# Layer norm rows and betas from VectorE to ScalarE, and old states added by TensorE as a product with the unit matrix

## The chip, the cores and the metric

The kernel runs on one core of a Trainium2 chip. The metric is the time on the device in microseconds; lower is better. The core has TensorE (matmuls, results to PSUM), VectorE and ScalarE (elementwise work on SBUF and PSUM), GpSimd (no PSUM) and SyncE (here only DMA issues). Each engine runs its own instructions in the order in which they are written, and they wait for each other by semaphores. All numbers are fp32.

## The reference, cut to what matters

```python
def _L0_attn_ref(x, ...):                      # x: layer normed, (2, 2048, 256); 16 heads of 64
    xn = layernorm(x) * ln_w + ln_b
    q, k, v = xn @ Wq.T, xn @ Wk.T, xn @ Wv.T
    alpha, aR = sigmoid(xn @ Wa.T + ba), sigmoid(xn @ WaR.T + baR)     # a gate for each key element
    beta, gamma = sigmoid(xn @ Wb.T + bb), sigmoid(xn @ Wg.T + bg)     # one for each head
    def step(carry, inp):                      # over the 2048 tokens
        S, R = carry                           # two states of 64x64 for each head
        kn = k_t / norm(k_t)
        r = clip(v_t - S.T @ kn, -1, 1)
        S = a_t[..., None] * S
        S = S + b_t * outer(kn, v_t - kn @ S)
        R = aR_t[..., None] * R
        R = R + g_t * outer(kn, r - kn @ R)
        return (S, R), S.T @ q_t + R.T @ q_t
    return os @ Wo.T + residual

x = x + _layernorm(_L0_attn_ref(_layernorm(x), ...))
x = x + _layernorm(_L0_ffn_ref(_layernorm(x), ...))   # router, 8 of 64 experts, and a shared expert
```

## The kernel before

The sequence is cut into 32 chunks of 64 tokens. A chunk holds both batches, so a tile has 128 rows. Within a chunk the recurrence is written as matrix products. With decayed keys it is solved by the inverse of a triangular 64x64 matrix for each head and state, then the states S and R (16 units of 128x64 each in SBUF) are carried to the next chunk. After attention come one last tile of routing and then the experts, 320 tiles in a pipeline of their own; the change doesn't touch the experts.

`attention` (from L490) writes out the program of each engine, chunk by chunk, in an order set by hand. While a chunk n is worked on, the front of chunk n+1 is made in the gaps: norm, projections, gates, keys, triangles A. The norms and the routing of the chunk n−1 run beside that.

PSUM has eight banks. `order_of_jobs` (L64) lists all results that go there in the order in which TensorE makes them. The table `SMALL` rotates through six banks, `WIDE` through two, and each names the engine that empties the bank. A result may begin only when the result six (or two) places ahead of it was emptied. By this list W follows six places behind U, RU behind SU, OUT behind the first half of RU, and the first half of V behind the second half of RU.

The parts of a chunk's end, in TensorE's order, with their names:

- U (L690) and PR, its product with the queries (L692). SU (L695) is the update of S, product of the keys kT and U. NS (L700) sums the squares of the next chunk's keys; ScalarE makes the norms of it in place (`key_norms`, L457), and VectorE multiplies the keys by them (L859).
- O (L702) is the output. Its first part uses the old S and R, and its end sets O_begun. SD is the shared expert. W (L711) is the solution for R, copied by ScalarE to B (L1049); with it O is finished (L713), and RU (L716) is the update of R.
- A (`triangles`, L591) are the triangles of the next chunk. VectorE masks them (`masked`, L758), ScalarE and GpSimd copy their diagonals to D (L922, L1063), and the next chunk's transposition (L778) needs these. RK ranks tokens for the routing, `route_pages` (L340) on VectorE follows it. OUT (L728) is the projection of the output and is added by VectorE to the residual (L887). V (L731) are the values of the next chunk.

VectorE adds SU to S after O_begun (L869) and RU to R (L878). ScalarE then multiplies each of 16 units by its decay (`decay_state`, L951): S after the copies of W and O, R behind the diagonals.

In the front half, from L778, VectorE inverts the triangles in 30 steps (`invert_steps`, L431), with other work set between them: four layer norms (y, the rows for the router, x of the chunk n+2, and xhat). Of each, VectorE makes the mean and the variance (`ln_stats`), ScalarE the inverse deviation by Ln and Exp (`ln_guess`, L916), and VectorE the row (`ln_apply`, L751). Between them stand the subtraction of KS, the masks of PQ (L809) and RQ, and the betas, 1 / (1 + exp) by an add and a reciprocal (L816). Its last step writes N (L827), for which TensorE's Z waits. ScalarE takes the exponentials of the gates (`exp_gate`, L929) and the copies of projections in this half; TensorE's projections rotate through the two wide banks, so each waits for ScalarE.

## Time and profile before

| | |
|---|---|
| median of three runs | 3295.07 us (3291.97 to 3296.05) |
| profiled execution | 3276.76 us, its span 3274.9 us |
| TensorE matmul busy | 2773.5 us, 85% |
| VectorE busy | 2721.3 us, 83% |
| ScalarE busy | 1943.8 us, 59% |
| GpSimd busy | 953.5 us, 29% |
| mean granted TensorE clock | 0.906 |

Attention fills the span up to some 2540 us, and the experts the rest from about 2620 us. The 40 slices of the page show VectorE at 8 to 9 tenths in nearly all of attention. A matmul's end is modelled, so TensorE's busy share is not its share at its peak. In timelines, a row has its start, its length, engine, line and names; "x2" says that two instructions are merged, and the bracket is the idle time of the engine ahead of it and who ended it. A matmul of fp32 shows as two instructions in the trace, so 32 matmuls of the program are x64 there.

### The profile page before, as it was taken

The numbers are of one execution on the slowest core, as the hardware profiler recorded it, in microseconds if no ns is written. First come the engines' busy times: TensorE is split into PE (matmuls) and PEld (weight loads), VectorE is DVE, ScalarE is ACT, GpSimd is POOL, SyncE is SP. The second block draws the span as 40 slices with busy tenths as digits, with TensorE's granted clock in tenths as the row PEclk, the third lists the DMA queues.
The fourth block names the chain that finished last, engine by engine and source line by source line (L and its number), as shares of the span: only waits on it lengthen the run. The fifth ranks groups of instructions, "written<-read, shape, count | busy, mean of one in ns | idle before, by whom it ended". The sixth has DMA issues, their size and how long they took to land. (4 is left out here: it accounts for less than half of the span.)

```text
span 3274.9 us, 132532 instructions
## 1 busy us (share of the span) xinstructions
PE 2773.5 (85%) x55642; PEld 2460.6 (75%) x55642; DVE 2721.3 (83%) x6827; ACT 1943.8 (59%) x5180; POOL 953.5 (29%) x928
## 2 busy tenths in 40 slices
PE   3888888888888888888888888888886199999986
PEld 3878888887787888788788888888786177777664
DVE  2889898888989988999999999999997156777776
ACT  2656555556666655666666555666654077666664
POOL 3112222222222222223222222233221101444444
PEclk8988898888888988989999899999998599999998
DMA  3321111111111111111111111111110945777776
GB/s 116 82 64 37 36 35 35 35 35 37 39 35 35 37 37 35 43 35 35 39 40 41 35 35 35 35 42 35 39 40 30 347 144 170 221 217 224 220 217 180
DMA packets 209563, 264.55 MB, mean 81 GB/s; under 512 B 30673, under 2 KB 183250, under 8 KB 208210
## 3 DMA queue, kind: packets, MB, share of 16 engines
q1 hardware_dynamic: 183936, 188.53, 19.0%
q0 software_dynamic: 24576, 67.27, 7.2%
q8 instruction: 450, 7.37, 1.0%
q14 instruction: 135, 1.11, 0.1%
q10 hardware_dynamic: 466, 0.27, 0.0%
HBM read 125.37 MB, written 130.58 MB: 78 GB/s over the span
## 5 line engine op out<-in xcount | busy, mean ns | idle before, releaser
L379 POOL DMA_INDIRECT table<-tail,places x256 | 277.1, 1082 | 721.1 <-DVE BR L852 214.8
L1496 PE MATMUL bank<-w,tail 128*128 x1280 | 357.2, 401 | 31.4 <-ACT tail L1539 14.5
L1468 POOL DMA_INDIRECT tail<-y_table,places x256 | 249.5, 975 | 449.3 <-DMA y_table<-tail 314.0
L1091 POOL COPY inv_r<-N 32x512 f32<-32x512 f32 x128 | 136.4, 1065 | 734.0 <-DVE N L827 730.0
L445 DVE TENSOR_TENSOR tri<-tri,step 128x58 f32<-128x58 f32 (+13 forms) x896 | 305.5, 341 | 30.8
L444 DVE TENSOR_TENSOR step<-tri 128x58 f32<-128x58 f32 (+13 forms) x896 | 301.4, 336 | 26.4
L1496 PEld LDWEIGHTS bank<-w,tail 128*128 128x128 f32 x1280 | 219.2, 191 | 95.9 <-issue 72.7
L1586 DVE TENSOR_TENSOR more<-tail 128x1 f32<-128x1 f32 x320 | 50.8, 159 | 193.7 <-ACT tail L1548 189.6
L1511 PE MATMUL bank<-w,tail 128*128 x640 | 191.1, 380 | 2.7 <-DVE tail L1597 1.4
L1546 ACT ACTIVATE tail<-bank 128x129 f32<-128x129 f32 x320 | 89.8, 281 | 158.9 <-PE bank L1496 156.3
L1482 PE MATMUL bank<-ident,tail 128*128 128x128 f32 x640 | 125.1, 278 | 66.1 <-DMA tail<-table 65.6
L587 PE MATMUL bank<-xnT,wa 128*128 128x128 f32 x992 | 125.3, 287 | 50.2 <-ACT xnT L970 50.2
L572 PE MATMUL bank<-B,kT_r 64*64 64x64 f32 x2048 | 107.2, 294 | 63.1 <-DVE S L869 63.1
L587 PEld LDWEIGHTS bank<-xnT,wa 128*128 128x128 f32 x992 | 119.4, 201 | 54.4 <-ACT xnT L970 54.4
L768 DVE TENSOR_TENSOR_SCAN c<-restart,z 128x1024 f32<-128x1024 bf16 x62 | 158.3, 2592 | 0.0
L1597 DVE TENSOR_SCALAR tail<-bank,more 128x256 f32<-128x256 f32 x320 | 152.1, 475 | 2.8 <-DMA y_table<-tail 2.1
L1482 PEld LDWEIGHTS bank<-ident,tail 128*128 128x128 f32 x640 | 78.8, 142 | 100.1 <-DMA tail<-table 78.3
L934 ACT ACTIVATE z<-bank,neg_bias 128x128 f32<-128x128 f32 x496 | 137.9, 374 | 27.0 <-PE bank L587 23.1
L572 PEld LDWEIGHTS bank<-B,kT_r 64*64 64x64 f32 x2048 | 102.3, 206 | 68.2 <-DVE S L869 68.2
L1539 ACT COPY tail<-bank 128x256 f32<-128x256 f32 x320 | 119.6, 374 | 56.7 <-PE bank L1482 56.0
L1068 POOL COPY T<-L_s 32x512 f32<-32x512 f32 x64 | 38.7, 605 | 368.2 <-DVE L_s L763 366.8
L955 ACT ACTIVATE S<-S,dec_end 128x64 f32<-128x64 f32 x512 | 125.8, 335 | 30.4 <-DVE S L869 30.4
(275 smaller groups left out, 8103.8 us busy)
## 6 DMA issues: line engine op xcount, KB each, us to landing
table<-blank SPq DMA_DIRECT2D x320, 128.5 KB, 3.2
tail<-table SPq DMA_DIRECT2D x320, 128.5 KB
y_table<-tail SPq DMA_DIRECT2D x320, 128.0 KB
w<-in_wpack_dram SPq DMA_DIRECT2D x16, 1540.0 KB, 19.3
tail<-in_x_dram SPq DMA_DIRECT2D x66, 64.0 KB, 2.5
x_rows<-tail SPq DMA_DIRECT2D x32, 128.0 KB
sh_rows<-tail SPq DMA_DIRECT2D x32, 128.0 KB, 1.9
table<-tail,places POOLq DMA_INDIRECT x256, 2.9
```

The lines of the kernel that those rows point to most:

```text
L379: nc.gpsimd.indirect_dma_start(out=table, out_offset=bass.IndirectOffsetOnAxis(ap=t.places[:, TOP * (n - 1) + k:TOP * (n - 1) + k + 1], ax ...
L444: link(nc.vector.tensor_tensor(step, s[:, 0:k, k:k + 1].broadcast_to([P, k, rest]), over(s[:, k, k + 1:Q], k), ALU.mult))
L445: link(nc.vector.tensor_tensor(s[:, 0:k, k + 1:Q], s[:, 0:k, k + 1:Q], step, ALU.add))
L572: mm = nc.tensor.matmul(ps[r, C * i:C * i + C], lhsT(r, u), rhs(r, u), start=(m == 0), stop=(m == len(pairs) - 1))
L587: mm = nc.tensor.matmul(ps[:, P * m:P * m + P], w[:, kt, P * hp:P * hp + P], t.xnT[:, kt, :], start=(kt == 0), stop=(kt == 1))
L768: nc.vector.tensor_tensor_scan(t.c[:, gate, :, :].rearrange("p u n -> p (u n)"), t.restart[:], t.z[:, gate, :], 0.0, ALU.mult, ALU.add).th ...
L934: ins = nc.scalar.activation(t.z[:, gate, P * hp:P * hp + P], ps[:, P * m:P * m + P], ACT.Exp, bias=t.neg_bias[:, gate, hp:hp + 1], scale= ...
L1468: nc.gpsimd.indirect_dma_start(out=t.term[2 * (m % 2) + k], out_offset=None, in_=d.y_table[0:P * closed(b) + P + 1, :], in_offset=bass.Ind ...
L1482: mm = nc.tensor.transpose(t.ps[T_bank[i % 2]][:, P * kt:P * kt + P], t.x_slot[i % X_RING][:, P * kt:P * kt + P], t.ident[:, :])
L1496: mm = nc.tensor.matmul(ps[:, 0:257], t.xT_slot[i % 3][:, P * kt:P * kt + P], weights(i, 257 * kt, 257), start=(kt == 0), stop=(kt == 1))
L1511: nc.tensor.matmul(t.ps[y_bank[i % 2]][:, 0:256], t.hT_slot[i % 3][:, :], weights(i, 514, 256), start=True, stop=True).then_inc(t.sem["y_d ...
L1597: nc.vector.tensor_scalar(t.y_slot[i % Y_RING], t.ps[y_bank[i % 2]][:, 0:256], t.share[:, i % 8:i % 8 + 1], None, ALU.mult).then_inc(t.sem ...
```

## The change

Five things are changed, all in attention but for the last, which the last routing tile uses too.

- SU and RU get a second term, the unit matrix times the old S or R, so that PSUM holds the new state before its decay. The adds of VectorE go.
- `decay_state` reads PSUM and writes the decayed unit to SBUF. It waits for O_begun, and a semaphore state_emptied counts the emptied halves. The decay of S moves ahead of the copies of W and O on ScalarE.
- `ln_guess` becomes `layer_norm` on ScalarE, which writes the row too: −mean, Ln, Exp, −mean times the inverse deviation, and Identity with scale and bias. VectorE waits for y_normed and res_ready.
- The betas are exp(−ln(1 + x)), on ScalarE, behind `gate_exp`.
- `count_pages` compares and adds all three sets of 64 columns at once, two instructions for three.

```diff
-         "KS": "dve", "KR": "act", "U": "act", "PR": "dve", "W": "act", "O": "out", "SU": "dve", "RU": "dve",
+         "KS": "dve", "KR": "act", "U": "act", "PR": "dve", "W": "act", "O": "out", "SU": "state", "RU": "state",
...
-def count_pages(nc, t, n):
-
-    for i in range(3):
-        ins = nc.vector.scalar_tensor_tensor(out=t.page_seen[:, i, :], in0=t.pages[n % 2][:], scalar=t.tile_of[:, i:i + 1],
-                                             in1=t.page_seen[:, i, :], op0=ALU.is_le, op1=ALU.add)
-    return ins
+def count_pages(nc, t, n, link):
+
+    link(nc.vector.tensor_tensor(t.page_hit[:], over(t.pages[n % 2][:], 3), bc(t.tile_of[:], E), ALU.is_le))
+    return nc.vector.tensor_tensor(t.page_seen[:], t.page_seen[:], t.page_hit[:], ALU.add)
...
-                    units(n, f"SU{h}", h, [(of(t.kT[0]), of(t.U))])
+                    units(n, f"SU{h}", h, [(of(t.kT[0]), of(t.U)), (lambda r, u: t.eye[r, :], of(t.S))])
...
-                    units(n, f"RU{h}", h, [(of(t.kT[1]), of(t.B))])
+                    units(n, f"RU{h}", h, [(of(t.kT[1]), of(t.B)), (lambda r, u: t.eye[r, :], of(t.R))])
...
-                link(ln_apply(2, norms + 1, t.y[:, :], t.y[:, :]))
+                dve.wait_ge(t.sem["y_normed"], n + 1)
...
-                ln_apply(3, norms + 2, t.xrow[n % 2][:, 0:256], t.y[:, :]).then_inc(t.sem["xf_ready"], 1)
...
-                    ln_apply(0, norms + 3, res[:, :], t.x_new[:, :]).then_inc(t.sem["res_ready"], 1)
                     dve.wait_ge(t.sem["res_ready"], n + 1)
...
-                    link(nc.vector.tensor_scalar(beta[:], t.bgz[:], 1.0, None, ALU.add))
-                    nc.vector.reciprocal(beta[:], beta[:]).then_inc(t.sem["beta_ready"], 1)
                 invert_steps(nc, t, link, 15, 20)
-                if ahead:
-                    wait_done(dve, t, o, n, "XT")
-                    ln_apply(1, norms + 4, t.xhat[:, :], t.res[(n + 2) % 3][:, :]).then_inc(t.sem["xhat_ready"], 1)
...
                 dve.wait_ge(t.sem["O_begun"], n + 1)
-                for h in range(2):
-                    ps = mm(n, f"SU{h}")
-                    nc.vector.tensor_tensor(t.S[:, half[h], :], blk(ps[:, :]), t.S[:, half[h], :],
-                                            ALU.add).then_inc(t.sem["dve_emptied"], 1)
...
-                for h in range(2):
-                    ps = mm(n, f"RU{h}")
-                    nc.vector.tensor_tensor(t.R[:, half[h], :], blk(ps[:, :]), t.R[:, half[h], :],
-                                            ALU.add).then_inc(t.sem["dve_emptied"], 1)
...
-            def ln_guess(i, order):
+            def layer_norm(i, order, dst, src):
+
+                tmp = t.ln_tmp[:, i, :]
                 act.wait_ge(t.sem["ln_var_ready"], order)
-                link(nc.scalar.activation(t.ln_tmp[:, i, 0:1], t.mv[:, i, 1:2], ACT.Ln, bias=t.tiny[:, 2:3]))
-                nc.scalar.activation(t.ln_tmp[:, i, 1:2], t.ln_tmp[:, i, 0:1], ACT.Exp,
-                                     scale=-0.5).then_inc(t.sem["ln_guess_ready"], 1)
+                nc.scalar.activation(tmp[:, 0:1], t.mv[:, i, 0:1], ACT.Copy, scale=-1.0)
+                link(nc.scalar.activation(tmp[:, 1:2], t.mv[:, i, 1:2], ACT.Ln, bias=t.tiny[:, 2:3]))
+                link(nc.scalar.activation(tmp[:, 1:2], tmp[:, 1:2], ACT.Exp, scale=-0.5))
+                link(nc.scalar.activation(tmp[:, 0:1], tmp[:, 0:1], ACT.Copy, scale=tmp[:, 1:2]))
+                return nc.scalar.activation(dst, src, ACT.Identity, bias=tmp[:, 0:1], scale=tmp[:, 1:2])
...
             def decay_state(n, g, state):
+                act.wait_ge(t.sem["O_begun"], n + 1)
                 for h in range(2):
-                    wait_emptied(act, t, o, n, f"{'SR'[g]}U{h}")
+                    ps = mm(n, f"{'SR'[g]}U{h}")
                     for u in range(8 * h, 8 * h + 8):
-                        ins = nc.scalar.activation(state[:, u, :], state[:, u, :], ACT.Copy,
+                        ins = nc.scalar.activation(state[:, u, :], ps[:, C * (u % 8):C * (u % 8) + C], ACT.Copy,
                                                    scale=t.dec_end[n % 2][:, g, u:u + 1])
-                ins.then_inc(t.sem["states_ready"], 1)
+                    ins.then_inc(t.sem["state_emptied"], 1)
+                wait_emptied(act, t, o, n, f"{'SR'[g]}U1")
+                act.sem_inc(t.sem["states_ready"], 1)
...
+                    link(nc.scalar.activation(t.bgz[:], t.bgz[:], ACT.Ln, bias=1.0))
+                    nc.scalar.activation(t.beta[(n + 1) % 2][:], t.bgz[:], ACT.Exp, scale=-1.0).then_inc(t.sem["beta_ready"], 1)
...
+                decay_state(n, 0, t.S)
                 for h in range(2):
                     empty(n, f"W{h}", even_odd(t.B, h))
                 for h in range(2):
                     act.wait_ge(t.sem["O_done"], 2 * n + h + 1)
                     nc.scalar.copy(by_pair(t.V[:], h), o.bank(t, n, f"O{h}")[:, :].rearrange("p (a b n) -> p a b n", b=2, n=C)).then_inc(t.sem["out_emptied"], 1)
-                decay_state(n, 0, t.S)
```

ScalarE at the end of a chunk, before: the copy of SD to the tile tail, W to B, O to V, the decays of S, and the diagonals to T.

```order
L1045 COPY tail<-bank 128x256 [waits sh_stored,front_mm]
L910 COPY B<-bank 128x8x64 [waits front_act,mm_done]
L910 COPY B<-bank 128x8x64 [waits mm_done]
L1052 COPY V<-bank 128x4x128 [waits O_done] x2
L955 ACTIVATE S<-S,dec_end 128x64 [waits dve_emptied]
L955 ACTIVATE S<-S,dec_end 128x64 x7
L955 ACTIVATE S<-S,dec_end 128x64 [waits dve_emptied]
L955 ACTIVATE S<-S,dec_end 128x64 x7
L926 COPY T<-L_s 32x512 [waits dve_emptied]
```

The same place of the changed kernel.

```order
L1025 COPY tail<-bank 128x256 [waits sh_stored,front_mm]
L931 ACTIVATE S<-bank,dec_end 128x64 [waits front_act,mm_done,O_begun]
L931 ACTIVATE S<-bank,dec_end 128x64 x7
L931 ACTIVATE S<-bank,dec_end 128x64 [waits mm_done]
L931 ACTIVATE S<-bank,dec_end 128x64 x7
L881 COPY B<-bank 128x8x64 [waits state_emptied,mm_done]
L881 COPY B<-bank 128x8x64 [waits mm_done]
L1033 COPY V<-bank 128x4x128 [waits O_done] x2
L901 COPY T<-L_s 32x512 [waits dve_emptied]
```

The sixteen decays of S now stand ahead of the copies of W.

TensorE from RU (B times kT_r) over the triangles (c, kplus) to OUT (wo, V), before.

```order
L572 MATMUL bank<-B,kT_r 64x64 [waits dve_emptied]
L572 MATMUL bank<-B,kT_r 64x64 x15
L572 MATMUL bank<-B,kT_r 64x64 [waits dve_emptied]
L572 MATMUL bank<-B,kT_r 64x64 x15
L549 MATMUL bank<-c,kplus 64x64 [waits out_emptied,plus_made]
L549 MATMUL bank<-c,kplus 64x64 x31
L549 MATMUL bank<-c,kplus 64x64 [waits act_emptied]
L549 MATMUL bank<-c,kplus 64x64 x31
L423 MATMUL bank<-tail 128x64 [waits sel_ready,front_act]
L424 MATMUL bank<-tail 128x64
L728 MATMUL bank<-wo,V 128x256 [waits out_emptied,dve_emptied]
```

The changed kernel: the end of RU, where pairs with R and the unit matrix (eye) alternate with the old ones, and what follows.

```order
L571 MATMUL bank<-B,kT_r 64x64 x2
L571 MATMUL bank<-R,eye 64x64 x2
L548 MATMUL bank<-c,kplus 64x64 [waits out_emptied,plus_made]
L548 MATMUL bank<-c,kplus 64x64 x31
L548 MATMUL bank<-c,kplus 64x64 [waits act_emptied]
L548 MATMUL bank<-c,kplus 64x64 x31
L422 MATMUL bank<-tail 128x64 [waits sel_ready,front_act]
L423 MATMUL bank<-tail 128x64
L727 MATMUL bank<-wo,V 128x256 [waits out_emptied,state_emptied]
```

RU has 64 matmuls where it had 32, and OUT waits for a decay by ScalarE where it waited for an addition by VectorE.

ScalarE ahead of the exponentials of the gates, before: two norms, each a Ln and an Exp on one column.

```order
L918 ACTIVATE tail<-tail,tiny 128x1 [waits ln_var_ready]
L919 ACTIVATE tail<-tail 128x1 [waits act_link]
L918 ACTIVATE tail<-tail,tiny 128x1 [waits ln_var_ready]
L919 ACTIVATE tail<-tail 128x1 [waits act_link]
L934 ACTIVATE z<-bank,neg_bias 128x128 [waits front_mm]
```

The changed kernel at this place.

```order
L891 ACTIVATE tail<-tail 128x1 [waits ln_var_ready]
L892 ACTIVATE tail<-tail,tiny 128x1
L893 ACTIVATE tail<-tail 128x1 [waits act_link]
L894 ACTIVATE tail<-tail 128x1 [waits act_link]
L895 ACTIVATE tail<-tail 128x256 [waits act_link]
L891 ACTIVATE tail<-tail 128x1 [waits ln_var_ready]
L892 ACTIVATE tail<-tail,tiny 128x1
L893 ACTIVATE tail<-tail 128x1 [waits act_link]
L894 ACTIVATE tail<-tail 128x1 [waits act_link]
L895 ACTIVATE res<-x_new,tail 128x256 [waits act_link]
L909 ACTIVATE z<-bank,neg_bias 128x128 [waits front_mm]
```

Four instructions have become ten, two of them on rows of 256 columns.

## Rows read from the trace of the kernel before

**Rows 1.** Windows: stretch, its length, busy us of each engine, clock, DMA share, GB/s.

```profile
core 0: us, PE busy (x) PEld busy (x) DVE busy (x) ACT busy (x) POOL busy (x), PEclk, DMA share, GB/s
108.00:2460.00 2352.00, 2066.04 (x50517) 1891.31 (x50515) 2131.30 (x4845) 1431.05 (x3346) 643.00 (x601) 0.90 0.13 39
```

**Rows 2.** Waits of VectorE, 200 to 2400 us: line, releaser, us, times, longest.

```profile
DVE k L859 <- ACT tri L460: 39.8, 29, 2.7
...
DVE L_s L763 <- PE bank L549: 14.0, 28, 1.1
DVE pqT L809 <- PE bank L644: 7.0, 20, 0.9
```

**Rows 3.** Timeline of TensorE, one chunk's end, and two later rows.

```profile
1063.27 3.04 PE L572 MATMUL bank<-U,kT_s 64*64 64x64 f32 x64
...
1073.58 1.16 PE L549 MATMUL bank<-BR,inv_r 64*64 64x64 f32 x64
1075.90 1.18 PE L549 MATMUL bank<-rqT,B 64*64 64x64 f32 x64 [1.16 <-ACT B L910]
1078.95 3.44 PE L572 MATMUL bank<-B,kT_r 64*64 64x64 f32 x62 [1.87 <-DVE S L869]
...
1082.24 2.21 PE L549 MATMUL bank<-c,kplus 64*64 64x64 f32 x126
...
1084.87 3.67 PE L728 MATMUL bank<-wo,V 128*128 128x256 f32 x16
...
1107.32 3.71 PE L644 MATMUL bank<-pq,c 64*64 64x128 f32 x64
...
1117.04 3.90 PE L572 MATMUL bank<-eye,c 64*64 64x64 f32 x128
```

**Rows 4.** Timeline of ScalarE, the same chunk's end and one row of the next.

```profile
1073.69 0.37 ACT L1045 COPY tail<-bank 128x256 f32<-128x256 f32 x1 [2.45 <-PE bank L416]
1074.77 1.07 ACT L910 COPY B<-bank 128x512 f32<-128x512 f32 x2 [0.71 <-PE bank L549]
...
1078.93 3.93 ACT L955 ACTIVATE S<-S,dec_end 128x64 f32<-128x64 f32 x16 [0.74 <-DVE S L869]
...
1086.23 1.24 ACT L926 COPY T<-L_r 32x512 f32<-32x512 f32 x2
...
1099.81 2.16 ACT L934 ACTIVATE z<-bank,neg_bias 128x128 f32<-128x128 f32 x8
```

**Rows 5.** Timeline of VectorE, the same stretch.

```profile
1071.34 1.23 DVE L859 TENSOR_TENSOR k<-k,tri 128x1024 f32<-128x1024 f32 x1 [1.92 <-ACT tri L460]
...
1081.78 1.45 DVE L878 TENSOR_TENSOR R<-bank,R 128x512 f32<-128x512 f32 x2
1083.63 1.29 DVE L763 TENSOR_TENSOR L_s<-bank,L_s 128x512 f32<-128x512 f32 x2 [0.40 <-PE bank L549]
...
1089.85 0.42 DVE L887 TENSOR_TENSOR tail<-bank,res 128x256 f32<-128x256 f32 x1
...
1091.18 1.99 DVE L778 STREAM_TRANSPOSE tri<-T 128x1024 f32<-128x1024 f32 x1
...
1109.57 2.48 DVE L809 TENSOR_TENSOR pqT<-bank,pq_mask 128x512 f32<-128x512 f32 x4
```

**Rows 6.** Groups by line, VectorE, 200 to 2400 us: busy, mean ns, idle before.

```profile
L755 DVE TENSOR_SCALAR tail<-tail 128x256 f32<-128x256 f32 x57 | 23.5, 413 | 2.2 <-DVE tri L445 0.2
L817 DVE RECIPROCAL beta<-beta 128x32 f32<-128x32 f32 x28 | 9.9, 353 | 1.0
```

**Rows 7.** Windows, four us in the next chunk's RU; columns as in rows 1.

```profile
1154.00:1158.00 4.00, 2.81 (x52) 2.81 (x54) 4.00 (x7) 3.24 (x13) 0.00 (x0) 0.53 0.09 19
```

**Rows 8.** Groups by line, ScalarE, 200 to 2400 us.

```profile
L918 ACT ACTIVATE tail<-tail,tiny 128x1 f32<-128x1 f32 x114 | 33.9, 297 | 138.0 <-DVE tail L749 138.0
L919 ACT ACTIVATE tail<-tail 128x1 f32<-128x1 f32 x114 | 23.1, 203 | 3.6
L970 ACT ACTIVATE xnT<-bank,lnb,lnw 128x128 f32<-128x128 f32 x58 | 22.9, 444 | 0.0
```

34 lines of the change are left out of this document (12 added, 22 removed).

## The prediction

> **What bounds the kernel now.** I read the windows first. Over the 32 chunks of attention VectorE is busy for 2131.3 of 2352 us, 91%, with TensorE at 88% and ScalarE at 61% [rows 1]. So VectorE looks like the bound and ScalarE like the engine with room, and the change moves work from the one to the other. One average over a chunk of some 76.7 us cannot say whether the room lies where the work goes, so I went on to VectorE's waits, which show where it is already late: 29 times for the key norms from ScalarE, 39.8 us in all and so 1.4 us a chunk; 28 times for the triangles A from TensorE, 0.5 us a chunk; 20 times for PQ, in 7.0 us together [rows 2]. All are small, and all sit at places where TensorE and ScalarE arrive just in time. The reader is to see three points of coupling; whatever is made later on those two engines ahead of one becomes idle time of VectorE at once.
>
> The last views are the timelines of one chunk's end on three engines [rows 3 to 5]. I call K the start of VectorE's product with the key norms (L859, 1071.34) and T the transposition that opens the next chunk (L778, 1091.18). T − K is 19.84 us. In it TensorE runs W (from 1073.58, done at 1074.74), waits for ScalarE's copy of W (1074.77 to 1075.84), finishes O (to 1077.08), waits until VectorE has added SU, and then runs RU (from 1078.95 to about 1082.3), the triangles A (to 1084.45) and OUT (1084.87 to 1088.54). VectorE masks A from 1083.63 and takes OUT at 1089.85, 1.3 us after it was done. That 1.3 us is all the cover OUT has.
>
> **Part 1: what VectorE is rid of.** The adds of S and R are two pairs, the R pair 1.45 us with its gap [rows 5], so some 2.6 us a chunk. Four norms of 256 columns go at 0.413 us each, 1.65 us, and the reciprocal of the betas at 0.353 us with an add ahead of it, 0.5 us [rows 6]. The page count has the same elements in two instructions in place of three: taken as nothing. Together 4.7 us a chunk, if no wait takes their place.
>
> **Part 2: the unit matrix term in SU.** SU has 64 matmul rows now and gets 128. The same shape and count, KT with the unit matrix, took 3.90 us at full clock, and SU took 3.04 us for 64 in a chunk where the clock was low [rows 3]. So the addition costs 1.95 us at the high clock and up to 3.4 us at the low one. I take 2.1, since TensorE is mostly at the high clock here. Nothing hides it: NS is queued behind SU on TensorE, ScalarE waits for NS and makes the key norms of it, and VectorE waits for these in 29 chunks out of 29 [rows 2]. K moves by **+2.1 us**. No work that VectorE is rid of lies between N and K, so nothing is given back there.
>
> **Part 3: from K to T.** Times here are after K; O_begun, SD and W follow NS on TensorE as before. W is done at K+3.4. ScalarE has copied SD at K+2.7 (1073.69 plus 0.37) [rows 4] and now does the 16 decays of S before the W copies. Their price from PSUM is not in the trace. Above stands 3.93 us, the same 16 out of SBUF. Below I use the copies of 512 elements, two in 1.07 us out of PSUM and two in 1.24 us out of SBUF [rows 4]: 0.085 us less each, 1.4 us less over 16, so 2.6 us. I take 3.5, nearer the row of the same function and shape. A page of the Trainium skill, "Perfetto Trace Analysis", section "Optimizing Scalar/DVE Operations", gives ScalarE an access overhead of about 93 ns on SBUF and 51 ns on PSUM. By it the 16 would take 3.93 − 16 × 0.042 = 3.3 us, and the whole sum would be some 9 us smaller; no row here shows it for this shape.
>
> Decays of S: K+2.7 to K+6.2. W copies to K+7.3, where they ended at K+4.5 before. TensorE ends O at K+8.5. RU then starts without waiting, since its banks were emptied by the decays, but it has 128 rows: 3.9 us at the high clock, 7.0 us at the low one (62 in 3.44 us) [rows 3]. The granted clock of the next chunk's RU stretch is 0.53, thus mostly 1.2 GHz, after a stretch in which TensorE waits [rows 7], and the waits ahead of it grow. I take 5.5, between the two: RU is done at K+14.0. Triangles A take 2.2 us: the first bank pair at K+15.1, the second at K+16.2. VectorE, which has finished its queries by K+9.3 (K+10.4 less the 1.2 us of adding S), sits idle until K+15.1, where it waited 0.4 us before. It masks until K+17.6 and ScalarE copies the diagonals (1.24 us for each pair) from K+16.4 to K+18.9.
>
> Now the second new wait: OUT takes the bank of RU0, and this is emptied by the first eight decays of R, which stand behind the diagonals on ScalarE. At 1.75 us for eight they end at K+20.7. OUT needs 3.7 us and is done at K+24.4. VectorE comes to the OUT addition at K+21.4 (6.2 us behind the first mask, 1083.63 to 1089.85, and a little for the second pair) and idles another 3 us. T follows 1.33 us behind the start of the OUT addition, with a little for its latency at K+25.85. Before it was K+19.84: **+6.0 us**, with the adds already taken off. The bounds: with RU at 3.9 us and the decays at their low price 3.1; with RU at 7.0 and decays of 3.93 us, 8.2.
>
> **Part 4: from T to N.** ScalarE's norm is now Copy, Ln, Exp, Copy, Identity where it was Ln and Exp (0.297 and 0.203 us) [rows 8]. The first Copy hides behind nothing but is short (0.1 us of issue), the second is about 0.3, and the Identity on 256 columns is between 0.444 (128 columns) and twice that; I take 0.55. With the links a norm grows by 1.0 us. Two norms stand ahead of the exponentials of the gates, which started at 1099.81 [rows 4]; VectorE hands over the variance 0.4 us earlier; so they start 1.6 us later, TensorE's r projections wait for the emptied bank (they already wait for it now), and PQ starts 1.6 us later than its 1107.32 [rows 3]. VectorE arrives at PQ, where it started at 1109.57 [rows 5], 1.2 us earlier and finds the last of four banks at 1112.6 instead of 1111.0; it leaves PQ 1.2 us later than before. Rid of the betas and of xhat it makes up 0.9, then meets RQ, which is 1.6 us later too, and reaches N some 1.1 us later. The sigmoid that stands on ScalarE ahead of N's copies adds about 0.5. Together **+1.6 us**. The lower bound is −2.1, when all that VectorE saves here counts (four norms and the betas); the upper one 2.5.
>
> **Sum.** 2.1 + 6.0 + 1.6 = 9.7 us a chunk. 31 chunks have a next one: 301 us; the last chunk has no masks or front, I count 3 us. Profiled execution: 3276.8 + 304 = 3581 us. The median of the runs is 3295.1, 18 us over the profiled one, and I let that stand: **3599 us**.
>
> **Rivals.**
> *Partial cover.* RU runs at the high clock (part 3 becomes 4.4) and VectorE's savings between T and N come through by half (−1.0). Then 2.1 + 4.4 − 1.0 = 5.5 a chunk, 3295 + 171 = 3466. For it speaks that SU is seldom at the low clock; against it the window at 0.53 [rows 7].
> *Low clock.* More waiting leaves TensorE at 1.2 GHz through SU and RU: 3.4 + 7.5 + 2.0 = 12.9, 3295 + 400 = 3695. For it speaks the same window, against it that the idle pieces are only some 3 us each.
> *VectorE is the bound and the covers hold (faster).* The 4.7 us come through: 3295 − 31 × 4.7 = 3149. The place is ScalarE between SD and W, K+2.7 to K+3.4: the decays of S cost nothing if they fit there, 0.7 us for sixteen, and OUT stays in time if RU is done by about K+11. Against it: one decay has a pitch of 0.24 us, so three fit. Faster than before as a whole would need parts 2 to 4 to be over 9.7 us too dear. The Trainium skill speaks for this rival: "Perfetto Trace Analysis", section "Identifying the Most-Contended Engine", says that the engine of highest occupancy is to be optimized first, and for VectorE that occupancy is a fair measure. The trace agrees on which engine that is, 91%, yet shows waits on others at three places.
>
> **How the numbers follow.** The forecast has 0.58, partial cover 0.20, low clock 0.16, the faster case 0.06. The range 3450 to 3710 takes in the first three with some 0.1 lost at their edges, and leaves out the fourth. About 0.2% can be told from no change by a measurement of this kernel: faster 0.05, same 0.01, slower 0.94.
>
> **What would show it.** Of each step in the changed profile: idle time of VectorE ahead of the key product of about 3.5 us a chunk (was 1.4); ahead of the first mask of A 5 to 6 us (was 0.5), ended by TensorE; new idle time ahead of the OUT addition of about 3 us (was none), with TensorE's OUT waiting for a decay of R; the W copies starting right behind the sixteenth decay of S; VectorE's wait for PQ at 1 to 2 us. VectorE's share falls from 91% to about 76%. It would be wrong if RU ended before K+12, if ScalarE's decays ran at half the pitch, or if the norms were so late that VectorE waited for a normed row as well, which would make it slower still.

## The result, and the profile after

The changed kernel is slower, by more than I had forecast.

| | before | after | forecast |
|---|---|---|---|
| median of the runs | 3295.56 us | 3688.40 us (3674.78 to 3697.87) | 3599 us (3450 to 3710) |
| ratio to before, 95% interval | 1 | 1.1185 (1.1144 to 1.1226) | 1.092 |
| profiled execution | 3276.76 us | 3686.63 us, its span 3684.8 us | 3581 us |
| mean granted TensorE clock | 0.906 | 0.881 | |

The first line to look at is the one that answers to [rows 1]: busy us of TensorE, its weight loads, VectorE, ScalarE and GpSimd over 31 chunks of attention, then the clock, in the changed kernel.

```profile
core 0: us, PE busy (x) PEld busy (x) DVE busy (x) ACT busy (x) POOL busy (x), PEclk, DMA share, GB/s
108.00:2870.00 2762.00, 2320.94 (x55056) 2116.95 (x55058) 2049.49 (x4617) 1543.71 (x3807) 657.10 (x613) 0.87 0.11 34
```

VectorE's share falls from 91% to 74%. The two stretches hold 30.5 and 31.0 chunks (2352 us by 77.1 and 2762 us by 89.0 a chunk, below), so its work is 69.9 us a chunk before and 66.0 after. No engine now has a share as high as VectorE's was: TensorE has 84%, ScalarE 56%. So the time is in waits. These are VectorE's, over 200 to 2800 us (line, what it waited for, us in all, times, longest), to be held against [rows 2]:

```profile
DVE L_s L755 <- PE bank L548: 160.8, 29, 6.5
DVE tail L858 <- PE bank L727: 156.9, 29, 5.8
DVE pqT L796 <- PE bank L643: 104.7, 111, 2.8
DVE k L838 <- ACT tri L459: 95.0, 29, 4.2
```

Per chunk VectorE waits 5.5 us for the triangles A (0.5 before), 5.4 us for OUT (a wait that before does not have), 3.6 us for PQ (7.0 us in all before) and 3.3 us for the key norms (1.4 before). TensorE, in turn, waits for ScalarE in two places that were not there or were short, 4.0 and 3.9 us a chunk (same stretch and columns):

```profile
PE bank L727 <- ACT R L931: 116.5, 29, 4.3
PE bank L548 <- ACT B L881: 112.9, 29, 4.1
```

So the engines wait in a ring: VectorE for TensorE, TensorE for ScalarE, at the places that the prediction named. The groups of TensorE by line and shape (busy us, mean ns of one, idle before it), 200 to 2800 us, show what the prediction left out:

```profile
L727 PE MATMUL bank<-wo,V 128*128 128x256 f32 x464 | 172.2, 551 | 116.5 <-ACT R L931 116.5
L643 PE MATMUL bank<-pq,c 64*64 64x128 f32 x1856 | 147.0, 330 | 0.0
```

An OUT matmul takes 551 ns. In the kernel before, the same product has a mean of 382 ns over its chunks:

```profile
L728 PE MATMUL bank<-wo,V 128*128 128x256 f32 x464 | 106.5, 382 | 0.0
L644 PE MATMUL bank<-pq,c 64*64 64x128 f32 x1792 | 113.7, 286 | 0.0
```

OUT's work is the same in both kernels. It costs 2.3 us more a chunk (172.2 less 106.5, over 29). What that is shows in one chunk's end of the changed kernel. As in the prediction, K is the start of the key product, 1207.35, and T the transposition that opens the next chunk, 1235.50. The timelines (start us, us, instruction, idle before) of ScalarE, TensorE and VectorE:

```profile
1208.96 3.39 ACT L931 ACTIVATE S<-bank,dec_end 128x64 f32<-128x64 f32 x16 [0.17 <-ACT tail L1025]
1212.46 1.07 ACT L881 COPY B<-bank 128x512 f32<-128x512 f32 x2
...
1223.46 1.24 ACT L901 COPY T<-L_s 32x512 f32<-32x512 f32 x2 [6.77 <-DVE L_s L755]
1224.72 1.24 ACT L901 COPY T<-L_r 32x512 f32<-32x512 f32 x2
1225.99 3.39 ACT L931 ACTIVATE R<-bank,dec_end 128x64 f32<-128x64 f32 x16
```

```profile
1213.59 1.99 PE L548 MATMUL bank<-rqT,B 64*64 64x64 f32 x64 [3.52 <-ACT B L881]
...
1220.92 2.03 PE L548 MATMUL bank<-c,kplus 64*64 64x64 f32 x126
...
1227.79 6.29 PE L727 MATMUL bank<-wo,V 128*128 128x256 f32 x16 [4.26 <-ACT R L931]
```

```profile
1207.35 1.23 DVE L838 TENSOR_TENSOR k<-k,tri 128x1024 f32<-128x1024 f32 x1 [3.31 <-ACT tri L459]
...
1222.14 1.29 DVE L755 TENSOR_TENSOR L_s<-bank,L_s 128x512 f32<-128x512 f32 x2 [5.45 <-PE bank L548]
...
1234.12 0.42 DVE L858 TENSOR_TENSOR tail<-bank,res 128x256 f32<-128x256 f32 x1 [5.74 <-PE bank L727]
...
1235.50 1.97 DVE L769 STREAM_TRANSPOSE tri<-T 128x1024 f32<-128x1024 f32 x1
```

TensorE stands idle 3.52 us until ScalarE has decayed S and copied W, then does the end of O in 1.99 us (1.18 in [rows 3]), and starts RU at the low clock. It waits 4.26 us for the first decays of R, then does OUT in 6.29 us (3.67 in [rows 3]). The windows of the same stretch have the granted clock in the eighth place: the wait with the start of the end of O, the first part of RU, the second part of RU, and OUT.

```profile
1212.00:1215.00 3.00, 1.41 (x52) 1.41 (x56) 3.00 (x4) 1.43 (x4) 0.00 (x0) 0.59 0.23 41
1215.00:1218.00 3.00, 3.00 (x74) 3.00 (x68) 1.69 (x3) 1.07 (x2) 0.00 (x0) 0.50 0.03 5
1218.00:1221.00 3.00, 3.00 (x94) 3.00 (x94) 0.00 (x0) 0.00 (x0) 0.00 (x0) 0.77 0.00 0
...
1226.50:1232.00 5.50, 4.21 (x10) 3.40 (x11) 1.72 (x10) 2.88 (x15) 0.00 (x0) 0.50 0.02 3
```

This chunk is one of the longer ones: over chunks 3 to 30 OUT takes 5.9 us in the mean, the end of O 1.8 and RU 5.2 (3.7, 1.2 and 3.5 in the kernel before).

To place the whole, I took the starts of three VectorE rows in every chunk (T, then N, the last step of the inversion, then K) and averaged the stretches between them. All kernels below are measured so, in us a chunk. T to N is the mean of all 32 chunks, of which the last is shorter, the rest of 31, so a row adds up to its last column within 0.2 us only:

| kernel | T to N | N to K | K to T | a chunk |
|---|---|---|---|---|
| before (first profile, another of the same kernel) | 34.7, 34.6 | 22.5, 22.3 | 19.8, 19.7 | 77.1, 76.6 |
| after | 36.7 | 24.1 | 28.0 | 89.0 |

In the changed kernel K to T has two values: 25.8 to 26.6 us in 6 of the 31 chunks and 27.6 to 29.1 in the other 25. The period of a chunk grows by 11.85 us.

### The profile page after: what moved, and what is told of

The parts are those of the page before. It is cut to its first block and busy times, and to the rows that moved or that the text cites. A ratio compares the mean times of both kernels' runs of the same rounds, so it can differ in the third digit from the quotient of the medians.

```text
span 3684.8 us, 140757 instructions
## 1 busy us (share of the span) xinstructions
PE 3018.5 (82%) x59738; PEld 2668.8 (72%) x59738; DVE 2594.8 (70%) x6481; ACT 2045.2 (56%) x5614; POOL 955.6 (26%) x928
## 5 line engine op out<-in xcount | busy, mean ns | idle before, releaser
L727 PE MATMUL bank<-wo,V 128*128 128x256 f32 x512 | 187.2, 544 | 124.7 <-ACT R L931 124.7
L1476 PEld LDWEIGHTS bank<-w,tail 128*128 128x128 f32 x1280 | 221.9, 193 | 90.1 <-issue 67.0
L727 PEld LDWEIGHTS bank<-wo,V 128*128 128x128 f32 x512 | 142.8, 286 | 160.5 <-ACT R L931 128.9
L1491 PE MATMUL bank<-w,tail 128*128 x640 | 196.4, 388 | 41.5 <-ACT tail L1534 30.5
L881 ACT COPY V<-bank 128x512 f32<-128x512 f32 x64 | 37.5, 586 | 256.6 <-PE bank L603 256.6
L755 DVE TENSOR_TENSOR L_s<-bank,L_s 128x512 f32<-128x512 f32 x64 | 41.2, 686 | 192.2 <-PE bank L548 192.2
L1491 PEld LDWEIGHTS bank<-w,tail 128*128 128x128 f32 x640 | 118.0, 190 | 74.0 <-issue 57.1
L796 DVE TENSOR_TENSOR pqT<-bank,pq_mask 128x512 f32<-128x512 f32 x128 | 88.2, 691 | 112.7 <-PE bank L643 112.0
L571 PE MATMUL bank<-B,kT_r 64*64 64x64 f32 x2048 | 163.3, 259 | 0.0
L643 PE MATMUL bank<-pq,c 64*64 64x128 f32 x2048 | 161.9, 330 | 0.0
L571 PE MATMUL bank<-R,eye 64*64 64x64 f32 x2048 | 160.5, 256 | 0.0
L548 PE MATMUL bank<-rqT,B 64*64 64x64 f32 x2048 | 57.2, 292 | 125.2 <-ACT B L881 125.2
```

The lines of the kernel that those rows point to most:

```text
L571: mm = nc.tensor.matmul(ps[r, C * i:C * i + C], lhsT(r, u), rhs(r, u), start=(m == 0), stop=(m == len(pairs) - 1))
L643: mm = nc.tensor.matmul(ps[r, 2 * C * m:2 * C * m + 2 * C], t.kminus[0][r, u, :], t.pq[r, :, u, :], start=True, stop=True)
L727: mm = nc.tensor.matmul(ps[:, 0:256], both, t.wo[:, hp, :], start=(hp == 0), stop=(hp == 7))
L1476: mm = nc.tensor.matmul(ps[:, 0:257], t.xT_slot[i % 3][:, P * kt:P * kt + P], weights(i, 257 * kt, 257), start=(kt == 0), stop=(kt == 1))
L1491: nc.tensor.matmul(t.ps[y_bank[i % 2]][:, 0:256], t.hT_slot[i % 3][:, :], weights(i, 514, 256), start=True, stop=True).then_inc(t.sem["y_d ...
```

## The experiments

Twelve runs were made, one of them of the kernel before itself. Ratios are to runs of the kernel before on the same chip; the interval is that of 95%. The chips differ: on one of them the kernel before has a median of 3313.53 us, against the 3295.56 us above. So kernels are best compared by ratio or by the us of a chunk.

### The two halves of the change apart

*states* has the change's part on the states alone: the unit matrix terms in SU and RU, no adds on VectorE, decays from PSUM with S ahead of the copies of W. *norms* has the other part alone: layer norm rows and betas on ScalarE, with the states as before.

```diff
 states, against before
+    units(n, f"SU{h}", h, [(of(t.kT[0]), of(t.U)), (lambda r, u: t.eye[r, :], of(t.S))])
...
     act.sem_inc(t.sem["sh_ready"], 1)
+    decay_state(n, 0, t.S)            # from PSUM
...
 norms, against before
+    layer_norm(2, norms + 1, t.y[:, :], t.y[:, :]).then_inc(t.sem["y_normed"], 1)
...
```

> The kernel before with the states' part of the change alone: unit matrix terms in SU and RU, decays from PSUM, the decay of S ahead of the copies of W; norms, betas and the page count stay as before. Theory 'two waits behind ScalarE' (the copies of W and OUT's bank): from N to the key product and from there to the next chunk's transposition the change cost 1.7 and 8.1 us a chunk by the two traces, and both stay, since neither lies at the norms: 31 x 9.8 = 304 us, 3600 us, in the range 3580 to 3620. Rival 'the norms on ScalarE delay everything': most of the loss goes with them, under 3450 us.

Measured: 3630.04 us, ratio 1.0959 (1.0898 to 1.1021).

> The changed kernel without the states' part: norms, betas and page count as changed, S and R added by VectorE as before. Theory 'the norms stand ahead of the gates' exponentials': 1.6 us a chunk from the transposition to N, as predicted, so 3345 us (3330 to 3360), with VectorE waiting at PQ for 1 to 2 us. Rival 'the front is late only because TensorE enters it at the low clock, after the states' waits': without them the matmul of PQ is as long as before (286 ns in the mean), VectorE's savings of 2 us outweigh the delay, and the time is 3280 to 3305 us.

Measured: 3379.83 us, ratio 1.0206 (1.0147 to 1.0265).

| kernel | T to N | N to K | K to T | a chunk |
|---|---|---|---|---|
| states | 34.4 | 24.5 | 27.9 | 86.9 |
| norms | 36.9 | 22.4 | 19.7 | 79.1 |

What follows: against the first profile the two halves cost 9.74 and 2.02 us a chunk, 11.76 together, and the whole change 11.85. That leaves nothing for an interaction, as far as the 0.5 us by which two profiles of the kernel before differ let one see. All of the loss from N to T belongs to the states, all from T to N to the norms. Both times lie over the ranges expected, by 10 and 20 us; by their ratios to 3295.56 us they would be 3612 and 3363 us, so most of that is the chip. Of these two runs, only the one with the norms has the wait for PQ. *norms* has it at 3.7 us a chunk (104.3 over 28 chunks); this is its row among VectorE's waits from 200 to 2400 us:

```profile
DVE pqT L796 <- PE bank L643: 104.3, 104, 3.5
```

Its PQ takes 323 ns a matmul (the mean of TensorE's group in the same stretch), that of *states* 271.

### The decays of R ahead of the diagonals

```diff
+                decay_state(n, 1, t.R)
                 if front:
                     diagonal(n, 0)
                     diagonal(n, 1)
-                decay_state(n, 1, t.R)
```

> The changed kernel with the decays of R moved ahead of the diagonals on ScalarE, nothing else. Theory 'OUT waits for the decays behind the diagonals, and this wait puts TensorE at the low clock': TensorE no longer waits ahead of OUT for over 1 us, OUT's matmuls go from 551 to some 380 ns, and the key product to the transposition falls from 28.0 to about 21.5 us: 3688 - 31 x 6.5 = 3487 us (3460 to 3520). Rival 'the low clock of OUT is from the wait for the copies of W, ahead of it': OUT stays at 540 ns and the gain is about 4.5 us a chunk, 3549 us. Rival 'RU1 and the diagonals on time decide': no gain, over 3650 us.

Measured: 3505.31 us, ratio 1.0584 (1.0523 to 1.0646), against 1.1185 of the change as it is. K to T falls from 28.0 to 22.8 us, with 21.5 expected, and T to N from 36.7 to 35.6. TensorE no longer waits ahead of OUT, and OUT is back at its time (group of TensorE, 200 to 2400 us):

```profile
L727 PE MATMUL bank<-wo,V 128*128 128x256 f32 x432 | 99.2, 382 | 0.0
```

What follows: the place of the R decays alone is worth 5.1 us a chunk from K to T, over half of what the states cost, and 6.1 us of the whole period. It is one line of the program. The wait and the slow OUT went together, so this run doesn't part the two.

### Matmuls of no use in TensorE's waits

This one parts them. TensorE gets 10 added matmuls of 128x256 behind W and 12 behind A, into a bank whose old content has been read. Nothing reads their results.

```diff
+            def warm(ps, count):
+                for m in range(count):
+                    nc.tensor.matmul(ps[:, 256:512], t.wo[:, 0, 0:P], t.wo[:, 0, :], start=True, stop=True)
...
                 crossed(n, "W", [(of(t.inv[1]), of(t.BR))])
+                if route:
+                    spare = begin(n, "RK")
+                    warm(spare, 10)
...
                     triangles(n)
                 if route:
-                    ps = begin(n, "RK")
+                    warm(spare, 12)
+                    ps = spare
```

> The changed kernel, with added matmuls of TensorE whose results nobody reads: 10 of 128x256 behind W, where TensorE waits for ScalarE's copy of W, and 12 of them behind the triangles A, ahead of the ranks, where it waits for the decays of R (with the first chunk as it was). The waits stay where they are, but the engine works in them. Theory (the part of K to T that I had sized too small is the low clock that a wait of 4 us leaves behind for the end of O, RU and OUT): OUT takes about 382 ns a matmul as in the kernel before, in place of 551, the time from K to T falls from 28.0 to 25.5 us a chunk, and the time by some 2.0 to 3.0 us a chunk, 3605 to 3630 us (ratio to before 1.094 to 1.10). Rival (the waits and the decays alone set the end, TensorE's clock only happens to be low beside them, or OUT's matmuls are slow for another reason): OUT stays near 550 ns or the end does not move, and the time stays at 3680 to 3710 us or rises by what the added matmuls delay.

Measured: 3618.68 us, ratio 1.0921 (1.089 to 1.0952). With more work to do, the kernel is some 70 us faster than the change as it is (87 us by the ratios, 2.5 us a chunk by the traces), in the middle of what the theory gave. The added work stands in one chunk's timeline of TensorE like this, with the end of O and OUT behind it:

```profile
1093.97 4.58 PE L580 MATMUL bank<-wo 128*128 128x256 f32 x20
1098.49 1.16 PE L548 MATMUL bank<-rqT,B 64*64 64x64 f32 x64
...
1106.20 5.45 PE L580 MATMUL bank<-wo 128*128 128x256 f32 x24
...
1111.88 3.67 PE L735 MATMUL bank<-wo,V 128*128 128x256 f32 x16
```

The end of O takes 1.16 us in place of 1.99 and OUT 3.67 in place of 6.29. Over all chunks OUT has 382 ns again and RU's matmuls 218 where the changed kernel has 258 (its groups over the same 200 to 2400 us; first the kernel with the added work, then the change):

```profile
L571 PE MATMUL bank<-B,kT_r 64*64 64x64 f32 x1664 | 98.5, 218 | 0.0
```

```profile
L571 PE MATMUL bank<-B,kT_r 64*64 64x64 f32 x1600 | 127.2, 258 | 0.0
```

K to T falls from 28.0 to 25.8 us, the period from 89.0 to 86.5. Over chunks 3 to 30, OUT is shorter by 2.3 us, and RU too is shorter, by 1.3 us (3.9 for 5.2). OUT begins no earlier for that, 20.6 us behind K in both kernels. So the price of the clock is more than these 2.2 us, since the second batch was longer than the wait it filled. The same chunk's row of ScalarE says so:

```profile
1108.83 3.38 ACT L939 ACTIVATE R<-bank,dec_end 128x64 f32<-128x64 f32 x16
```

Half of the 16 decays are done at 1108.83 + 1.69 = 1110.52, and OUT could have begun then; it began at 1111.88, so 1.36 us were lost to the added work. The rival, that the waits and decays alone set the end, is out. The first batch shows the cost of such a filling too: the end of O starts 0.6 us later than in the changed kernel, runs faster, and ends where it did.

### The decays of S: behind the copies, and half and half

```diff
 s_decay_back, against after
-                decay_state(n, 0, t.S)
                 for h in range(2):
                     empty(n, f"W{h}", even_odd(t.B, h))
...
+                decay_state(n, 0, t.S)
                 if front:
                     diagonal(n, 0)
...
 s_half, against r_decay_first
-                decay_state(n, 0, t.S)
+                decay_state(n, 0, t.S, [0])     # the first half only
                 for h in range(2):
                     empty(n, f"W{h}", even_odd(t.B, h))
+                decay_state(n, 0, t.S, [1])
```

> The changed kernel with the decays of S back behind the copies of W and O on ScalarE, where they stood before; nothing else. Theory 'RU needs SU's bank, so the decays of S are on the path wherever they stand': the copies of W come 3 us earlier, but RU then waits for the decays of S and ends at the same place, 3675 to 3700 us. Rival 'their place ahead of W is the cost': RU starts 2.7 us earlier, 3688 - 31 x 2.7 = 3604 us.

Measured: 3725.12 us, ratio 1.124 (1.1175 to 1.1305), which can't be told from the change's 1.1185 (1.1144 to 1.1226); K to T 28.6 us, no better. The decays of S left the way of W, and stood in the way of RU, whose banks they empty. Two rows of TensorE's waits, 200 to 2400 us:

```profile
PE bank L571 <- ACT S L931: 70.1, 25, 2.8
...
PE bank L548 <- ACT B L881: 28.6, 25, 1.5
```

> The changed kernel with the decays of R ahead of the diagonals (as in r_decay_first), and the 16 decays of S parted: the eight of the first bank stay ahead of ScalarE's copies of W, the eight of the second follow the copies of W and stand ahead of those of O. Theory (what the decays of S hold up costs one for one on the path W copy, end of O, RU, A): eight decays are 1.7 us, so the time from K to T falls from 22.8 to about 21.1 us a chunk, and the whole from 3505 to 3450 us (ratio 1.042). VectorE's wait for A falls by 1.5 us a chunk or more. Rival (RU cannot start before the second half is decayed anyway, or the copies of O, which now come later, hold up OUT): within 10 us of r_decay_first, 3495 to 3515 us.

Measured: 3430.48 us, ratio 1.0345 (1.0317 to 1.0374). K to T falls from 22.8 to 20.0 us, 2.8 where I had expected 1.7 for eight decays. TensorE's wait for the copy of W is 2.0 us a chunk, 3.9 in *r_decay_first* (row of its waits, 200 to 2400 us), and RU's matmuls fell from 263 to 235 ns:

```profile
PE bank L548 <- ACT B L881: 54.5, 27, 2.3
```

What follows: what stands ahead of the copy of W is paid one for one, and the work behind the shorter wait runs faster on top. Over chunks 3 to 30 the end of O begins 1.9 us earlier behind K, and it and RU take 1.3 us less (6.0 for 7.3). With two placements mended, K to T is where it was before the change (19.8), and what is left of the loss is SU's term from N to K and the norms.

### The key norms' squares ahead of SU

NS, for which VectorE is late in 29 of 29 chunks [rows 2], stands behind SU on TensorE. Here it goes ahead, in the changed kernel (*ns_ahead*) and in the kernel before (*before_ns*). Only the order of two blocks changes.

```diff
-                for h in range(2):
-                    units(n, f"SU{h}", ...)
                 if front:
                     pe.wait_ge(t.sem["keys_squared"], n + 1)
...
+                for h in range(2):
+                    units(n, f"SU{h}", ...)
```

> The changed kernel with NS set ahead of SU on TensorE, behind the product of U and the queries; nothing else. The key product K then comes some 3.3 us earlier after N, since VectorE waited that long for the norms. Theory 'from U on it is TensorE's and ScalarE's chain over SU, O, W, RU and A that sets the transposition T, and K lies beside it': the same work stands between U and W in another order, so what N to K loses K to T gains, and the time stays within 10 us of the changed kernel's (3688 us where before is 3296 us, so a ratio of 1.116 to 1.122). Rival 'the key norms are on the path, as the prediction had it': 31 x 3.3 = 100 us less, ratio 1.088.

Measured: 3710.0 us, ratio 1.1249 (1.1225 to 1.1272), a little over the 1.116 to 1.122 of the theory. N to K falls by 2.8 us, from 24.1 to 21.4, and K to T grows by 3.3, from 28.0 to 31.3. Of the 0.5 us by which the second is more, SU, which now runs behind NS, takes some 0.4 (4.3 us over chunks 3 to 30 in place of 3.9). VectorE's wait moved from the key product to the masks of A (waits, 200 to 2400 us):

```profile
DVE L_s L755 <- PE bank L548: 219.5, 25, 10.5
...
DVE k L838 <- ACT tri L459: 8.1, 17, 0.5
```

> The kernel before with NS set ahead of SU on TensorE, nothing of the change. Theory 'in the kernel before the key norms are on VectorE's path': its wait of 1.4 us a chunk for them goes, all behind K is VectorE's own work, and RU, which waits for VectorE's addition of SU, comes earlier too: up to 31 x 1.4 = 43 us less, ratio 0.987 to 0.993. Rival 'O and W, later by nothing, hold VectorE at the masks of A instead': no change, ratio 0.998 to 1.002.

Measured: 3278.76 us, ratio 0.9928 (0.9913 to 0.9943). In the kernel before, the same move is a gain: N to K is 21.2 us in place of 22.3 to 22.5, K to T stays at 19.65, and the wait for the key norms is nearly gone (39.8 us in [rows 2]; waits, 200 to 2400 us):

```profile
DVE k L859 <- ACT tri L460: 8.9, 19, 0.5
```

What follows: the gain of an earlier start is kept only where the next thing VectorE needs is not late as well. In the changed kernel TensorE and ScalarE set the time of A, and VectorE merely waits in another place.

### The norms' place on ScalarE, and PQ's clock

*norms_order* puts ScalarE's copies of the transposed row ahead of the norm of y, and the exponentials of the first gate ahead of the next two norms. *norms_bg* leaves the order of the norms and moves BG, a product with a result of 16 columns that stands just ahead of PQ, behind PQ, with ScalarE's work on it.

```diff
 norms_order, against norms
-                layer_norm(2, norms + 1, t.y[:, :], t.y[:, :]).then_inc(t.sem["y_normed"], 1)
                 ...                       # XT copies
+                layer_norm(2, norms + 1, t.y[:, :], t.y[:, :]).then_inc(t.sem["y_normed"], 1)
+                if front:
+                    exp_gate(n, 0)
                 layer_norm(3, norms + 2, ...)
...
 norms_bg, against norms (BG of both engines, behind PQ)
-    jobs = [("XT", "")] * front + ... + two("r") * front + [("BG", "")] * front
+    jobs = [("XT", "")] * front + ... + two("r") * front
+    jobs += [("RT", "")] + [("PQ", str(i)) for i in range(4)] + [("BG", "")] * front + two("k") * front + ...
```

> The run 'norms' (norms, betas and page count on ScalarE, states as before) with another order on ScalarE: the copies of xnT first, then the norm of y, then the exponentials of the first gate, then the two norms of the router's rows and of the next x. Theory 'the norms cost only by standing ahead of xnT and the gates': TensorE's front starts 1 to 1.5 us earlier after T than in the kernel before, VectorE's savings come through, T to N falls from 36.9 to about 33 us, and the time is 31 x 1.7 = 50 us under that of before (ratio 0.980 to 0.992). Rival 'VectorE stays bound by PQ, whose matmuls fall to the low clock whenever VectorE is ahead': PQ stays at 320 ns, T to N at 34.5 or more, ratio 0.998 to 1.01.

Measured: 3356.17 us, ratio 1.017 (1.0151 to 1.019), against 1.0206 (1.0147 to 1.0265) of *norms* on another chip: no difference that the intervals part. The first projection is at full clock again (278 ns, 349 in *norms*), and PQ is slower, 357 ns in place of 323. T to N is 36.1 us against 36.9, and 34.7 before the change. The theory had 33 us and a gain, so it failed. Its rival, VectorE bound by a slow PQ, is nearer, though PQ is slower than its 320 ns and the ratio is over its 1.01.

> The norms and betas part of the change alone (as in norms), with TensorE's gate product BG (matmuls with a result of 16 columns) and ScalarE's exponential of it and the betas moved from behind the r projection to behind PQ, ahead of the k projection and its copies. Theory (PQ falls to the low clock because TensorE waits for ScalarE around BG, just ahead of PQ): PQ returns to some 280 ns a matmul from 323, the time from T to N falls from 36.9 to 35.5 us a chunk, the whole by 30 to 45 us to about 3340 (ratio 1.008 to 1.012). Rival (the waits for ScalarE at the first projections alone leave the clock low, whatever stands between them and PQ): PQ stays at 315 ns or over, and the time within 10 us of the 3380 of norms, or above it where the later BG holds up the k projection.

Measured: 3366.73 us, ratio 1.0153 (1.0125 to 1.0181). The theory is half right. PQ returned to full clock, and the k projection, which now stands behind BG, went to the low one; it has 278 ns in *norms*. Groups of TensorE, 200 to 2400 us:

```profile
L641 PE MATMUL bank<-pq,c 64*64 64x128 f32 x1792 | 103.9, 271 | 0.0
...
L586 PE MATMUL bank<-xnT,wk 128*128 128x128 f32 x896 | 146.5, 341 | 0.0
```

The time from T to N stays at 36.8 us, because VectorE's wait moved from PQ to RQ, which comes behind the k projection (waits, 200 to 2400 us):

```profile
DVE rqT L803 <- PE bank L571: 115.3, 56, 4.2
```

What follows: with the norms on ScalarE, moving BG moved the low clock from the product that had stood behind it to the one that now does. BG's place alone does not make it, though. In *r_decay_first* BG and the norms are as in the changed kernel, and PQ has 273 ns where that has 330; *states*, with BG ahead of PQ too, has 271 (group of *r_decay_first*, 200 to 2400 us):

```profile
L643 PE MATMUL bank<-pq,c 64*64 64x128 f32 x1664 | 98.1, 273 | 0.0
```

What lowers the clock there, BG's small matmuls or the waits around them and ahead of them, these runs leave open. The norms' loss from T to N is no VectorE work but time that TensorE and ScalarE need; a new order on one engine moved the wait, not the end.

### What is worth keeping

*pick* is the kernel before with NS ahead of SU, RQ ahead of the k projection on TensorE, and of the change only what I took to be covered: ScalarE makes the norm of y behind the XT copies, the norm of xhat and the betas. The norms of the router's rows and of the next x stay on VectorE; the states are as before.

```diff
+                for h in range(2):
+                    units(n, f"RQ{h}", h, [(of(t.kminus[1]), of(t.rqplus))])
                 if front:
                     for i in range(2):
                         projection(n, f"k{i}", t.wk, i)
...
-                ln_guess(2, norms + 1)
                 ...                       # ScalarE: XT copies
+                layer_norm(2, norms + 1, t.y[:, :], t.y[:, :]).then_inc(t.sem["y_normed"], 1)
                 ln_guess(3, norms + 2)
...
-                    ln_guess(1, norms + 4)
+                    layer_norm(1, norms + 4, t.xhat[:, :], t.res[(n + 2) % 3][:, :]).then_inc(t.sem["xhat_ready"], 1)
```

> The kernel before with NS moved ahead of SU on TensorE (as in before_ns) and of the change only what I expect to be covered: the norms of y and of xhat and the betas on ScalarE, with ScalarE's copies of the transposed row first, and RQ ahead of the k projection on TensorE; the norms of the router's rows and of the next x stay on VectorE, the states as before. Theory (work moved to ScalarE pays where it is queued behind nothing that TensorE waits for): VectorE is rid of two norms and the betas, 1.3 us a chunk, of which most comes through: 3240 to 3260 us, ratio 0.980 to 0.988. Rival (T to N is set by TensorE and ScalarE here, not by VectorE's own work): the same time as before_ns within 10 us, 3270 to 3290, or slower by what the norm of y adds ahead of the gates' exponentials, up to 3310.

Measured: 3249.13 us (3245.36 to 3260.32), ratio 0.9807 (0.978 to 0.9834). It beats both kernels. A chunk takes 74.95 us (33.9, 21.6, 19.4), against 75.7 of *before_ns* (34.8, 21.2, 19.7). The windows' row, 31 chunks of attention, has VectorE at 92% (91% before the change), with the clock at 0.93:

```profile
108.00:2420.00 2312.00, 2085.48 (x50906) 1894.88 (x50906) 2123.43 (x4795) 1502.88 (x3618) 651.13 (x609) 0.93 0.14 40
```

What follows: this part of the change, set at places that I took to be covered, comes with a gain of 1.2% over *before_ns* by the ratios (0.9807 and 0.9928) in place of a loss. Whether the gain comes from the norms or from RQ's new place was not parted, so that the norms pay by themselves is not shown.

### The kernel before, once more

> The kernel before, unchanged, for a second trace of it. In its first trace the experts, from the first load of a tile on, took 638 us, while in the traces of the changed kernel and of four variants, with the same code there, they took 676 to 682. Theory 'their length changes from one execution to the next': this one shows 650 to 680 us for the same kernel. Rival 'the change makes the experts slower, by what attention leaves behind': 635 to 645 us again.

Measured: 3311.75 us, a single run. A chunk takes 76.6 us, against 77.1 in the first profile. What differs is the part behind attention; the point on the frame, below, takes it up.

## Why the prediction was right and where it was wrong

The direction and the mechanism were right: two new waits behind ScalarE's decays, VectorE idle at the masks and at OUT. The size was 89 us too small, with the result near the upper end of the range. By the terms of the sum, in us a chunk:

| term | forecast | measured |
|---|---|---|
| part 2, N to K | 2.1 | 1.7 |
| part 3, K to T | 6.0 (3.1 to 8.2) | 8.1 |
| part 4, T to N | 1.6 (−2.1 to 2.5) | 2.0 |
| sum | 9.7 | 11.8 |

**Part 1.** VectorE's work fell by 3.9 us a chunk (69.9 to 66.0) where I had 4.7. Waits took the place of all of it.

**Part 2.** SU takes 3.9 us over chunks 3 to 30, where it took 2.4 before. That is 1.5 us more, under the 1.95 to 3.4 that I set, because the old SU was in part at the low clock and the new one is hardly (its U matmuls have 227 ns, 243 before). VectorE waits 3.3 us for the key norms; I had said about 3.5. The view behind [rows 2] has a further wait between N and K, of the VectorE step that writes BR, for TensorE: 35.5 us, 25 times. I had not named it. It is 28.8 us, 30 times, in the changed kernel over 200 to 2800 us, so it took no part in the loss.

**Part 3, the step that failed.** The marks of the typical chunk above, against those of the prediction, in us behind K:

| | forecast | measured |
|---|---|---|
| decays of S begin, end | 2.7, 6.2 | 1.6, 5.0 |
| copies of W end | 7.3 | 6.2 |
| end of O | 8.5 | 8.2 |
| RU done | 14.0 | 13.6 |
| first mask of A | 15.1 | 14.8 |
| OUT begins | 20.7 | 20.4 |
| OUT done | 24.4 | 26.7 |
| T | 25.85 | 28.15 |

Up to the start of OUT each mark is right within 1.2 us, and within 0.4 us from the end of O on. Some of that is luck: in this chunk ScalarE was done with SD 1.3 us earlier than in the chunk that I had read, and the end of O, which I had priced at 1.2 us, took 1.99 at the low clock; the two nearly cancel. RU took about the 5.5 us that I had given it, between its prices at the two clocks. Sixteen decays from PSUM were sized at 3.5 us and took 3.39. The Trainium skill, "Perfetto Trace Analysis", section "Optimizing Scalar/DVE Operations", gives ScalarE access overheads of about 93 ns on SBUF and 51 ns on PSUM, and the estimate worked out from them was 3.3. The trace agrees within 0.1 us. Then the step "OUT needs 3.7 us and is done at K+24.4": OUT took 6.29 us, 2.6 us too much, at a granted clock of 0.50 for most of it. I had read a stretch at the low clock behind a wait of TensorE [rows 7], and had applied it to RU. I predicted a second wait of some 4 us right ahead of OUT, and gave OUT the price that it has without one. Over the chunks this is 2.3 us, which covers the 2.1 that part 3 lacked (8.1 less 6.0). So the two waits and their places were right, and the failed term of the sum is OUT's 3.7 us. The run with the added matmuls shows the cause: TensorE was kept at work where it would have waited, OUT took 3.67 us again, and the kernel got faster by doing more.

**Part 4.** The exponentials of the gates began at T+10.2, as predicted (1068.27 in a chunk with its T at 1058.11). VectorE's wait for PQ was to be 1 to 2 us and is 3.6, because PQ too went to the low clock, 330 ns against 286, or 1.0 us more a chunk (147.0 over 29 against 113.7 over 28). This I had not foreseen. At N only 0.4 us of it is left (2.0 against 1.6); which of VectorE's lighter work took up the rest was not tested.

**The frame.** The part behind attention is unchanged code, and its loads took 40.7 us more in the profile after than in the profile before. The loads of the experts' tiles span 637.6 us in the profile before and 678.3 in the one after, as the rows of that transfer show (kernel before, the kernel before once more, and after; the last numbers are first and last start):

```profile
L1432 SPq DMA_DIRECT2D tail<-table x320: 319/320/4833, 2597.1 to 3234.7; - x160
```

```profile
L1432 SPq DMA_DIRECT2D tail<-table x320: 319/320/4832, 2582.4 to 3270.6; - x160
```

```profile
L1412 SPq DMA_DIRECT2D tail<-table x320: 319/320/4830, 2967.6 to 3645.9; - x160
```

In twelve further profiles, the second of the kernel before among them with 688.2, it was 675.3 to 688.2 us. The profile before was the odd one, and the second profile of the same kernel shows that the change did not make the difference. Why that one execution was shorter is not known. I had put 18 us between the profiled execution and the median. So of the 89 us that the forecast lacks, about 67 are attention (370.5 measured to the first load, 304 forecast) and about 23 this frame.

**The rivals.** *Low clock* at 3695 us came closest in time, and its name is right, its place not: it put SU at the low clock (3.4 us) and RU at 7.0 us. SU's term cost 1.7 us from N to K and RU took 5.4; the clock fell at OUT and PQ. In part its nearness is luck, since it has 400 us for attention, where 370.5 were measured, and the frame, which is no part of that case, makes up most of the difference. *Partial cover* had RU at the high clock, 3.9 us, and a gain of 1.0 us from T to N, where the measured is a loss of 2.0. The *faster* case needed the decays of S to fit into 0.7 us on ScalarE; they took 3.4 and each held up the copy of W. The rule behind that case, in the Trainium skill's "Perfetto Trace Analysis", section "Identifying the Most-Contended Engine", names the engine with the highest occupancy as the one to optimize first. By it that is VectorE (91%), yet taking 3.9 us of work a chunk off it came with a loss of 12% here, and 92% is VectorE's share in the fastest kernel of the study. The share said which engine was busiest, and the waits said what the relief would cost.

## What to carry to other kernels

Work moved from the busiest engine to one with room is priced by what it is queued ahead of, not by the room: here 16 short instructions ahead of a copy, and 16 behind two others, made most of 12% (8.1 of 11.85 us a chunk, and with both placements mended K to T is back at 20.0). Where a step brings a wait of some 4 us to TensorE, price the matmuls right behind that wait at the low clock, each time and not only at the first place (551 ns an OUT matmul here for 382). The 4 us are what was seen here and no threshold: in the kernel before, RU stands behind waits of 1.2 and 1.9 us [rows 3], and its matmuls have 302 ns, where 218 is what they have with TensorE kept at work. And check how an in-order bank rotation ends: a result that takes the bank of a state's update inherits every delay of the engine that empties it.
